# Reciprocals spread through DRAM and a projection in three fp32r products, in a two-layer attention kernel

## The reference, cut to what matters

```python
qkv = jnp.einsum('oc,bchw->bohw', w_qkv, x)                 # the projection, 256 -> 768 channels
qkv_ms = jnp.concatenate([qkv, _aggreg(qkv, w_dw, w_pw)], axis=1)   # 5x5 depthwise, then 8x8 in groups
# 64 heads of 8 channels each, q = relu(q), k = relu(k), v1 = v and a row of ones:
vk = jnp.einsum('bhdn,bhen->bhde', v1, k)
out = jnp.einsum('bhde,bhen->bhdn', vk, q)
out = out[:, :, :-1] / (out[:, :, -1:] + EPS_ATT)           # the division by the denominator
out = jnp.einsum('oc,bchw->bohw', w_proj, out)
# batch norm over all images, times gamma, plus beta, plus x
```

## Time and profile before

| what | value |
|---|---|
| median of 3 runs | 2346.55 us (2340.79 to 2351.91) |
| the profiled execution, own time | 2353.07 us |
| its span, first to last instruction | 2351.3 us |
| TensorE busy | 2133.4 us, 91% |
| VectorE busy | 1530.9 us, 65% |
| ScalarE, GpSimd busy | 833.4 us, 214.3 us |
| mean granted clock of TensorE | 0.955 of full speed |
| DMA traffic | 448.14 MB, mean 191 GB/s |

### The profile page before, as it was taken

How to read it: one execution, slowest core, us unless ns; L and a number is a source line. 1 busy time by engine, 2 the same in 40 slices (tenths; PEclk the granted TensorE clock), 3 DMA queues, 4 the chain that set the end, 5 groups by cost and what they waited for, 6 DMA issues and landing times. The chain is left out here.

```text
span 2351.3 us, 31988 instructions
## 1 busy us (share of the span) xinstructions
PE 2133.4 (91%) x12680; PEld 1513.9 (64%) x12680; DVE 1530.9 (65%) x2330; ACT 833.4 (35%) x1807; POOL 214.3 (9%) x207
## 2 busy tenths in 40 slices
PE   6999999999698799999999999999999999999810
PEld 6888888889566466666666656666666665665500
DVE  4667766767418849667676794975866679491452
ACT  4434434344233333332342332333333233333142
POOL 2233122331100000000000000000000000000000
PEclk9999999999899899999999999999999999999865
DMA  2201222020376864865686486486577658646578
GB/s 105 81 41 41 81 81 81 1 81 41 126 265 214 289 213 159 287 229 209 231 279 213 181 277 224 173 285 226 197 255 254 206 190 270 223 176 222 231 324 358
DMA packets 137411, 448.14 MB, mean 191 GB/s; under 512 B 6960, under 2 KB 105904, under 8 KB 119216
## 3 DMA queue, kind: packets, MB, share of 16 engines
q1 hardware_dynamic: 136112, 427.24, 51.1%
q0 software_dynamic: 1152, 18.87, 1.9%
HBM read 271.30 MB, written 174.78 MB: 190 GB/s over the span
## 5 line engine op out<-in xcount | busy, mean ns | idle before, releaser
L745 PE MATMUL cv<-work,wc 128*64 128x288 f32 x4608 | 620.4, 414 | 22.6 <-issue 18.4
L745 PEld LDWEIGHTS cv<-work,wc 128*64 128x64 f32 x4608 | 307.7, 137 | 267.9 <-issue 53.3
L726 PE MATMUL pj<-x,wqkv 128*128 128x288 f32 x1536 | 389.4, 410 | 20.3 <-DMA x<-scratch_x 20.3
L726 PEld LDWEIGHTS pj<-x,wqkv 128*128 128x128 f32 x1536 | 288.7, 191 | 114.0 <-issue 39.8
L1130 DVE STREAM_SHUFFLE spun<-work 128x1152 f32<-128x1152 f32 x240 | 345.2, 1444 | 0.1
L955 ACT ACTIVATE work<-cv 128x288 f32<-128x288 f32 x384 | 158.0, 411 | 514.6 <-PE cv L745 508.9
L1136 DVE SCALAR_TENSOR_TENSOR spun<-work,spun 128x1152 f32<-128x1152 f32 x240 | 321.2, 1343 | 0.0
L1111 DVE TENSOR_TENSOR wc<-taps 128x512 f32<-128x512 f32 x288 | 180.3, 689 | 194.9 <-PE cv L745 182.4
L936 ACT COPY work<-pj 128x288 f32<-128x288 f32 x384 | 153.6, 400 | 289.5 <-PE pj L726 288.9
L1164 DVE TENSOR_TENSOR q<-q,tr 128x384 f32<-128x384 f32 x180 | 92.2, 550 | 93.8 <-PE tr L837 93.8
L853 PE MATMUL cv<-q,mt 128*128 128x384 f32 x384 | 127.9, 486 | 1.0 <-DVE q L1164 1.0
(11 more groups left out here) (112 smaller groups left out, 2996.8 us busy)
## 6 DMA issues: line engine op xcount, KB each, us to landing
work<-scratch_padded SPq DMA_DIRECT2D x48, 2599.5 KB, 10.6
scratch_padded<-work SPq DMA_DIRECT2D x48, 1300.0 KB, 6.5
scratch_phases<-work SPq DMA_DIRECT2D x96, 576.0 KB, 5.1
work<-scratch_phases SPq DMA_DIRECT2D x64, 576.0 KB, 5.2
x<-scratch_x SPq DMA_DIRECT2D x9, 2304.0 KB, 10.4
scratch_x<-xs SPq DMA_DIRECT2D x8, 2304.0 KB, 6.9
q<-scratch_phases SPq DMA_DIRECT2D x32, 576.0 KB, 4.6
xs<-in_x SPq DMA_DIRECT2D x7, 2304.0 KB, 9.1
```

The source lines that it names most:

```text
L726: mm = nc.tensor.matmul(pj[:, c % 2, :PLANE], wqkv[:, kc, u, :], x1[:, kc, c * PLANE:(c + 1) * PLANE], start=(kc == 0), stop=(kc == CT - 1))
L745: mm = nc.tensor.matmul(cv[64 * b:64 * b + 64, j % 2, :PLANE], wc[:, 2 * j + b, dy].rearrange("p c o -> p (c o)"), window, start=(dy == 0) ...
```

## The change: what it does

The spread by products goes, and with it `spread`, `rhi`, `rlo` and `SPREADS`. SP stores the reciprocals to a DRAM tensor `recip` (two DMAs for each pair of chunks), and loads them back eightfold into a tile of 128 rows and 1536 columns in SBUF, six loads an image (the ones for source 1 in two DMAs each), two buffers in turn. VectorE multiplies q by these six tiles, all after the second half of unit 1's weights. The last image uses other memory that is free by then.

The projection multiplies fp32r parts: hi by hi, hi by lo, lo by hi, 48 products a unit. The weights are split once, at the start. x is split for each image: ScalarE casts four quarters under unit 4's convolution, GpSimd subtracts (VectorE for image 0). The low part lies in the place of x1, so the last image's x1 is loaded again for `phase_out`.

The replica is read back in halves into a ring of three (`rep`, `ring`), each half when its place is free, where it was two whole buffers. `phase_out` stores its output from ScalarE's queue, each store behind the scaling of the next image, and no longer from GpSimd's.

```diff
-        wqkv = sb("wqkv", [P, CT, NU, P])
+        whi = sb("w1hi", [P, CT, NU, P], F32R)
+        wlo = sb("w1lo", [P, CT, NU, P], F32R)
-        qpad, rep, kva, stage, vkraw = cut(work, (2, QPAD), (2, NB * PADDED + ROW), (2, HW), (2, HB // 2, PLANE), (2, P + 1))
+        qpad, rep, kva, stage, vkraw = cut(work, (2, QPAD), (3, HB * PADDED + ROW), (2, HW), (2, HB // 2, PLANE), (2, P + 1))
+        bcb = sb("bcb", [P, 2, 4 * CHUNK])
...
+            def replica(i, u, h):
+
+                n = i * NU + u
+                size = HB * PADDED + ROW - 1 if h == 0 else HB * PADDED - 1
+                sp.wait_ge(padded_out[u % 2], (n // 2 + 1) * 16)
+                if 2 * n + h >= 3:
+                    sp.wait_ge(cv_filled, (n - 1) * NG + (4 if h else 0))
                 rows = dram["padded"][u % 2]
+                sp.dma_start(rep[:, ring(n, h), 0:size], bass.AP(
+                    rows.tensor, rows.offset + h * HB * PADDED, [[NB * PADDED, P // 2], [1, 2], [1, size]])).then_inc(rep_in[ring(n, h)], 16)
...
+            def store_reciprocals(i, d):
+
+                sp.wait_ge(r_ready, i * NDEN + d + 1)
+                wait_count(sp, bc_freed, NCH * i)
+                for source in range(2):
+                    sp.dma_start(dram["recip"][d, source].rearrange("h r n -> r h n"),
+                                 rcp[64 * source:64 * source + 64, (d % 2) * CHUNK:(d % 2 + 1) * CHUNK]).then_inc(rc_out[d], 16)
+
+            def load_reciprocals(i, n):
+
+                d, source = n // 2, n % 2
+                sp.wait_ge(rc_out[d], 32 * (i + 1))
+                if i != last_image:
+                    wait_count(sp, bc_freed, NCH * i + (n - 1 if n >= 2 else 0))
+                elif n == 2:
+                    sp.wait_ge(cv_filled, NIMG * NU * NG)
+                    sp.wait_ge(pj_filled, NIMG * NU * NG)
+                    sp.wait_ge(vkd_ready, 2 * NIMG - 1)
+                rows, tile = dram["recip"][d, source], bc_tile(i, n)
+                if source == 0:
+                    sp.dma_start(tile, bass.AP(rows.tensor, rows.offset, [[0, DIM], [4 * CHUNK, NB], [1, 4 * CHUNK]])
+                                 ).then_inc(bc_in[n], 16)
+                else:
+                    for h in range(2):
+                        sp.dma_start(tile[h:P:2], bass.AP(rows.tensor, rows.offset + HB * h * 4 * CHUNK, [
+                            [4 * CHUNK, HB], [0, DIM], [1, 4 * CHUNK]])).then_inc(bc_in[n], 16)
...
-                    lay_store(i, u)
+                    lay_store(i, u, [0])
+                    if u + 1 < NU or nxt:
+                        replica(*unit_at(i, u + 1), 1)
+                    if u == 1 and i:
+                        load_reciprocals(i - 1, 4)
+                        load_reciprocals(i - 1, 5)
+                    lay_store(i, u, [1])
...
+                    if u == 0 and i:
+                        for d in range(NDEN):
+                            store_reciprocals(i - 1, d)
+                        load_reciprocals(i - 1, 0)
+                        load_reciprocals(i - 1, 1)
...
                     if u + 2 < NU or nxt:
                         replicate(*unit_at(i, u + 2))
+                    if u == 0 and i:
+                        load_reciprocals(i - 1, 2)
+                        load_reciprocals(i - 1, 3)
...
-                        mm = nc.tensor.matmul(pj[:, c % 2, :PLANE], wqkv[:, kc, u, :],
-                                              x1[:, kc, c * PLANE:(c + 1) * PLANE],
-                                              start=(kc == 0), stop=(kc == CT - 1))
+                        high, low = (a[:, kc, c * PLANE:(c + 1) * PLANE] for a in (xhi[:], xlo[:]))
+                        nc.tensor.matmul(pj[:, c % 2, :PLANE], whi[:, kc, u, :], high, start=(kc == 0), stop=False)
+                        nc.tensor.matmul(pj[:, c % 2, :PLANE], whi[:, kc, u, :], low, start=False, stop=False)
+                        mm = nc.tensor.matmul(pj[:, c % 2, :PLANE], wlo[:, kc, u, :], high, start=False, stop=(kc == CT - 1))
...
-                pe.wait_ge(bc_freed, 4 * NCH * (i + 1))
...
                 for c in chunks:
+                    pe.wait_ge(bc_freed, NCH * i + 2 * (c // 2 + 1))
...
+                        if u == 4 and nxt and j in (2, 4, 6):
+                            high(i + 1, j // 2 - 1)
+                    if u == 4 and nxt:
+                        high(i + 1, 3)
...
+            def normalize(i, ns):
+                for n in ns:
+                    d, source = n // 2, n % 2
+                    dve.wait_ge(bc_in[n], (16 + 16 * source) * (i + 1))
+                    qc = q[:, 2 * source:2 * source + 2, d * 2 * CHUNK:(d + 1) * 2 * CHUNK]
+                    nc.vector.tensor_tensor(qc, qc, bc_tile(i, n).rearrange("p (j n) -> p j n", j=2), ALU.mult
+                                            ).then_inc(bc_freed, 1)
...
-                    normalize(i - 1, range(12))
                 weights(i, 1, [1])
                 if prev:
-                    normalize(i - 1, range(12, 4 * NCH))
+                    normalize(i - 1, range(NCH))
                 weights(i, 2)
...
+            def store_out(k):
+
+                act.wait_ge(summed, k + 1)
+                act.dma_start(dram["out"][order[k]], buffers[k % NB][0]).then_inc(store[k % NB], 16)
```

More of the change, by code:

```diff
@@ L43 @@
 WINDOW = PY * ROW
+HALF = HB * PADDED + ROW
+XPART = HW // 4
 DT, AG = -(-NG * PADDED // P), HW // (2 * P)
@@ L512, in _, with phase_l1 @@
                     image(2 * it + par, par)
-def phase_l1(nc, dram, sem, bnst, q, x1, work, early):
+def phase_l1(nc, dram, sem, bnst, q, x1, xhi, xlo, work, early, x_again):
     with ExitStack() as ctx:
@@ L570, in phase_l1 @@
+        bc_in = [sem(f"l1_bc_in{n}") for n in range(NCH)]
+        NFIRST, NW = 1, 4
         last_image = NIMG - 1
         NDEN = NCH // 2
-        NREP, NLAY = 16, 16
+        NLAY = 16
         Y_CHUNKS = {1: (0, 1), 2: (2, 3), 3: (4, 5)}
-        SPREADS = {(0, 5): range(0, 2), (0, 6): range(2, 5), (0, 7): range(5, 8),
-                   **{(1, j): range(8 + 2 * j, 10 + 2 * j) for j in range(NG)}}
-        spread_raw = stage.rearrange("p h j n -> p (h j n)")[:, 0:8 * P].rearrange("p (c j h) -> p c j h", c=2, j=4)
@@ L604, in groups_of, with bc_tile @@
             return DG if PRODUCTS[p][1] == 0 else AG
-        def bc_bank(i, k):
-            return (cv if i is last_image and k % 4 >= 2 else tr)[:, k % 2]
+        def bc_tile(i, n):
+            if i == last_image and n >= 2:
+                spare = (wc.rearrange("p b y c o -> p (b y c o)"), spun.rearrange("p t n -> p (t n)"),
+                         whi[:].bitcast(F32).rearrange("p k u m -> p (k u m)"))[0 if n < 4 else n - 3]
+                first = (n % 2) * 4 * CHUNK if n < 4 else 0
+                return spare[:, first:first + 4 * CHUNK]
+            return bcb[:, n % 2]
         def y_bank(k):
@@ L695, in _ @@
             replicate(0, 0)
+            replica(0, 0, 1)
             replicate(0, 1)
@@ L698, in _ @@
                 image(i, i + 1 < NIMG)
+            for d in range(NDEN):
+                store_reciprocals(last_image, d)
+                load_reciprocals(last_image, 2 * d)
+                load_reciprocals(last_image, 2 * d + 1)
             sp.wait_ge(y_out, 16 * len(Y_CHUNKS) * (NIMG - 1))
@@ L919, in _, with high @@
         def _(act):
+            act.wait_ge(w_first, 16 * NFIRST)
+            nc.scalar.copy(whi[:], wqkv).then_inc(w_split, 1)
+            def high(i, s):
+                act.wait_ge(x_in, 16 * (i + 1))
+                nc.scalar.copy(x_part(xhi, s), x_part(x1, s)).then_inc(xhi_ready, 1)
+            for s in range(4):
+                high(0, s)
             act.wait_ge(zeroed, 1)
@@ L1052, in _ @@
             project_product(last_image, 3)
-            for d in range(NDEN):
-                round_reciprocals(last_image, d)
             output(last_image, range(NCH))
@@ L1094, in _ @@
                     masked(i - 1, 3)
-                    attend(i - 1)
                 for p in range(3):
                     masked(i, p)
+                if i != last_image:
+                    for s in range(4):
+                        low(i + 1, s)
             masked(last_image, 3)
-            attend(last_image)
         @block.vector
         def _(dve):
+            dve.wait_ge(w_split, 1)
+            nc.vector.tensor_tensor(wlo[:], wqkv, whi[:].bitcast(F32), ALU.subtract).then_inc(w_split, 1)
+            for s in range(4):
+                dve.wait_ge(xhi_ready, s + 1)
+                nc.vector.tensor_tensor(x_part(xlo, s), x_part(x1, s), x_part(xhi, s).bitcast(F32),
+                                        ALU.subtract).then_inc(xlo_ready, 1)
             def weights(i, u, halves=range(2)):
@@ L1210, in _, with phase_out @@
                 image(i, True)
-            reciprocals(last_image, 0)
-            reciprocals(last_image, 1)
-            normalize(last_image, range(8))
-            reciprocals(last_image, 2)
```

(29 more changed lines are left out.)

139 lines of the change are left out of this document (56 added, 83 removed).

## The result

The changed kernel takes 2544.06 us (median of 4 runs, 2541.77 to 2560.69) where the kernel before takes 2346.59 beside it: ratio 1.0856 [1.0829, 1.0884]. The prediction was 2338, with 2236 to 2375 as its range: wrong in sign and far outside. C (slower, at 2380) has the right place and a fraction of the size.

What follows compares the result with a forecast made beforehand. TensorE, busy 91% of the span, was taken as the bound, DMA in the output stage. Six whole images -10, first -6, last -1, start 0, tail +8: together -9 us from 2346.6, so 2338; range 2236 to 2375.

Steps and rivals of the forecast that it cites:

- C: Rival: eight engines reading the same few rows make broadcast loads dearer; at 4.8 us a load +33, 2380; chance 0.12.
- The DRAM trip: Reciprocals stored and loaded back: TensorE waits 14.8 us an image before unit 2's convolution.
- the price of the ring: DMA ring, first in, first out: 3.8 us a broadcast load on eight engines, 3.2 a half replica, at 415 GB/s.
- the list: Timed steps of the trip in one image, from denominators ending at 22.1 us to unit 2's weights at 79.0.
- the clock after the long gap: TensorE runs at the lower level for a while after the wait before unit 2: 1.9 us charged.
- Projection: 48 fp32r products a unit take 6.55 us where 7.8 before: 1.25 less a unit, 7.5 an image.
- hidden: Split of x by ScalarE casts and GpSimd subtractions of 2.6 us each, covered by convolutions; 3 us an image if uncovered.
- VectorE late once: Weights of unit 5, behind VectorE's shuffles for units 2 and 3, come 1.4 us late; 1.5 charged in images 0 to 6.
- Spreads taken out: Spread products leave unit 2's projections (4.3 us) and unit 1's convolutions (8.1): 12.4 us less an image, in seven images.
- Tail: Last image's outputs end within 1 us of before; output stage's early loads stand behind the last trip: 8 us more.

Runs made afterwards that it cites:

- experiment 3: The changed kernel with its broadcast loads reading distinct rows of x1, 8 still outermost, instead of repeated reciprocals: 2523.07 us, 21 less than the change.
- 10: The changed kernel with source 0 loads read with 16 rows outermost, each repeated eight times: 2472.14 us, 1.0533 to the kernel before.
- experiment 11: The changed kernel with a third place for reciprocals, in VectorE's shuffle buffer: 2517.79 us, 1.0734 to the kernel before.
- experiment 9: Projection and ring of three without the trip, VectorE's turns reordered, last k and v pair's product one step later: 2287.74 us, 0.9751 to the kernel before.
- experiment 1: The changed kernel with reciprocals spread by products as before, keeping the new projection and the ring of three: 2348.45 us, 1.0011 to the kernel before.

## Why the prediction was wrong

**The step that failed is "The DRAM trip", and in it the price of the ring.** It took 3.8 us for each load, by half of the engines at the 415 GB/s of the earlier trace rows, and 3.2 for a half replica. The half of the engines was right (share 0.51). The rate was not, for the three loads of source 0: with nothing beside it, one moved 123 GB/s at a share of 0.51, 241 for a full ring, and with the replica the ring made 243. Of the 18.5 us by which unit 2's convolution comes after the forecast, load 0 carries 3.0 (8.9 less the 5.9 at its issue), load 2 with the half replica 5.3 and load 4 2.8: 11.1 together. Part of this could be read before: 415 is the output stage's, and the phase that was costed made 337. But at 337 a load is 4.7, 0.9 more, and the loads of source 1 came at about 3.8 all the same (the padded store was charged 3.8, where its bytes at 415 are 3.2, and took 3.7); the 3 to 5 are a price of this pattern that no row of before holds. Rival C named these loads, but as a rise of 1 us in each of six. Its reason, that the engines read the same rows, is not borne out for them: with distinct rows the loads of source 0 were as late (experiment 3), and what helped was sixteen engines (10: 72 us less).

**A wait was missed.** `rcp` has two places and three reciprocals go through it. The third must wait until the stores of the first have landed, and SP's third pair of stores waits for the third. The changed kernel has it (`rc_out` in `reciprocals`), and the list took the reciprocals as 3.1 us each with nothing between. It measured 5.4 in this image and 2.9 to 5.4 in all seven, worth 26 us (experiment 11).

**The consequences of a later ring.** Behind the half replica nothing new failed, but the output of chunks 0 and 1 also waited (2.79 us), and the clock after the long gap is 0.58 in it and 0.95 in the stretch behind it, where 1.9 us were charged. An image is 218 us where 192.2 were forecast: 15.2 by the wait, 2.8 by the output, 4.9 by unit 5 and the projection (below), and the other 3 lie in slower records after the gaps, which nothing here isolates.

**Projection: right in size, and its cover wrong.** A unit takes 6.5 us, as forecast, and nothing was wrong with 1.25 a unit (between 0.12 and 0.17 the pace of 288 columns would have been 0.1325, not 0.1335; the products start 0.1355 apart); experiment 9 has 59 us of the 60. (Its order of turns was not tried on the kernel before, but the image of the earlier trace rows had only 0.8 us of idle TensorE to win.) But the split was costed at nothing, "hidden" by GpSimd's idle time. The cover was asked for the engine that does it, and not for its neighbour: VectorE, with no slack ahead of unit 5, pays 5.3 us an image for 12.5 us of subtractions. "VectorE late once" had the right place (the weights of unit 5) and 1.5 us for what was 5.8 in experiment 1 and 4.5 in the change.

**Spreads taken out: right** (they are gone, and the stretches are shorter by it: TensorE is ready at 67.5 less the output's 2.8, 64.7, where 64.2 was forecast). **Tail: mis-sized.** SP's timeline of the last image:

```profile
2363.39 0.62 SPq L714 DMA_DIRECT2D bcb<-scratch_recip  x1
...
2365.37 1.16 SPq L699 DMA_DIRECT2D scratch_recip<-work  x2
2380.42 0.61 SPq L714 DMA_DIRECT2D wc<-scratch_recip  x1
...
2397.50 0.61 SPq L714 DMA_DIRECT2D spun<-scratch_recip  x1
...
2402.55 0.52 SPq L779 DMA_DIRECT2D y_third<-scratch_y  x1
```

And when VectorE could use the first pair:

```profile
2372.93 1.76 DVE L1217 TENSOR_TENSOR q<-q,bcb 128x1536 f32<-128x1536 f32 x1 [6.31 <-DMA bcb<-scratch_recip]
2378.78 1.76 DVE L1217 TENSOR_TENSOR q<-q,bcb 128x1536 f32<-128x1536 f32 x1 [4.09 <-DMA bcb<-scratch_recip]
```

A pair of loads comes 17 us after the pair before, not 7.6: the pair lands 15.4 after its issue, the next stores stand in the ring behind it, and the next loads wait for those stores. From the first denominator to TensorE's end it is 79.0 us (56.2 before), +22.8 where the outputs were put within 1 us. The output stage itself is +3.8.

The whole: +2.7 up to the first denominator (forecast -6, with the first image), +147.5 in six images (-10), +16.0 in the last (-1), +22.8 and +3.8 in the tail (+8): 192.8, and the spans differ by 192.9.

## What to carry to other kernels

Price a transfer at what the ring moved in the stretch where it will stand (its GB/s over its share there), not at the best rate of the trace. A load whose pattern stands nowhere in the trace, as an eightfold one on half of the engines, has no price there: run that one pattern before a plan is built on it. Work "hidden" on an idle engine is hidden only if the engine beside it, which may be held up, has slack; ask that of GpSimd and VectorE each time. When a saving does not show, look for the queue that was just in time before: here nearly all of the projection's 60 us were there once a few lines of order were moved.

## What the runs showed of the hardware

- A product of VectorE over 1152 columns (1.34 us) took 2.3 to 3.7 us while GpSimd subtracted, and always ended 1.21 to 1.22 us after the subtraction that was under way; the subtractions took 2.6 to 3.8 us; VectorE's shuffles stayed at 1.42 to 1.50 (experiment 1). The Trainium skill, GPSIMD Engine Reference, Specifications: GpSimd shares its SBUF interfaces with VectorE, and contends with instructions of VectorE that have two SBUF inputs. The products have two and the shuffles one; the trace agrees.
- A load whose outermost dimension is 8 kept half of the DMA engines busy (0.51, 191 GB/s). The Trainium skill, DMA: Bandwidth & Descriptors, Rules for kernel authors, says that an outermost dimension below 16 confines a DMA to at most that many engines, and the trace agrees.
- Such a load can be dearer than its share of engines: one with its eight copies outermost moved 123 GB/s at a share of 0.51 with nothing beside it, and took 9.4 to 9.5 us from issue to use; with 16 rows outermost 5.9 to 6.0, with 128 distinct ones 4.7 to 4.8. Why stays open.
- Engines that look busy can move little: 224 to 243 GB/s for a full share, at shares of 0.87 to 1.04, with the eightfold loads beside the replica halves, 351 with 128 (64) distinct rows outermost. Experiments 3 and 10 each removed one of the two suspects and neither restored it. Why stays open.
- A small DMA waits for the large ones ahead of it in its queue: two stores of 96 KB behind two loads of 768 KB let the next loads go only 15 us later (2365.37 to 2380.42), 1.6 us after the second load was used.
